# Taking the row maximum of attention scores over pairs of keys, with a ReLU on ScalarE and a joint add and maximum on VectorE

## What is computed

```python
def _L1_attn_ref(x, Wq, bq, Wk, bk, Wv, bv):
    q = jnp.einsum('bsd,ed->bse', x, Wq) + bq
    k = jnp.einsum('bsd,ed->bse', x, Wk) + bk
    v = jnp.einsum('bsd,ed->bse', x, Wv) + bv
    scale = 1.0 / jnp.sqrt(jnp.float32(x.shape[-1]))
    scores = jnp.einsum('bqd,bkd->bqk', q, k) * scale
    attn = jax.nn.softmax(scores, axis=-1)
    return jnp.einsum('bqk,bkd->bqd', attn, v)
...
x = x + _L0_conv_ref(_gn(x), L0_conv_weight)
t = _to_tokens(x)
t = t + _L1_attn_ref(_ln_t(t), ...)
t = t + _L1_ffn_ref(_ln_t(t), ...)
```

## Time and profile before

| | us |
|---|---|
| median of 3 runs | 3349.98 (3346.87 to 3349.98) |
| the profiled execution | 3355.51 |
| its span | 3353.4 |
| PE, DVE, ACT, POOL busy | 2829.6, 2110.8, 1417.5, 1017.1 |
| attention of the 56 chunks | about 204 to 2925 of the span |

### The profile page before, as it was taken

One profiled execution on the slowest core, in us unless ns is written; L12 is line 12 of the kernel. 1 busy time (PEld: TensorE's weight loads), 2 busy tenths in 40 slices (PEclk: granted clock), 3 DMA queues, 4 the chain that ended last, 5 costly groups with the idle time before them and its releaser, 6 DMA issues.

```text
span 3353.4 us, 46969 instructions
## 1 busy us (share of the span) xinstructions
PE 2829.6 (84%) x14124; PEld 1813.3 (54%) x14124; DVE 2110.8 (63%) x5723; ACT 1417.5 (42%) x3153; POOL 1017.1 (30%) x1185
## 2 busy tenths in 40 slices
PE   2489999999999999998999899998999898867660
PEld 1345555555666655655556566565665555545540
DVE  2466667667767777668666776777766766443331
ACT  0024443444454544554444454554455455523320
POOL 2000001222112224243242433423323432467445
PEclk9679999999999999999999999999999999955555
DMA  4100000001111111111111111111111111123321
GB/s 98 46 16 16 16 15 19 21 21 26 31 40 35 34 43 42 47 42 42 45 41 46 44 40 47 43 36 42 40 41 36 33 40 37 39 65 71 73 56 31
DMA packets 275327, 134.01 MB, mean 40 GB/s; under 512 B 225040, under 2 KB 268816, under 8 KB 275088
## 3 DMA queue, kind: packets, MB, share of 16 engines
q1 hardware_dynamic: 245168, 101.06, 12.2%
q0 software_dynamic: 29920, 29.94, 4.2%
HBM read 84.24 MB, written 46.66 MB: 39 GB/s over the span
## 4 chain that ended last, share of the span: by engine, by line
PE 61%; DVE 22%; issue 6%; POOL 5%; ACT 3%; DMA 2%; SPq 1%; POOLq 0%; DVEq 0%; ACTq 0%
PE ps_o L1095 16%; PE ps_s L1082 8%; DVE max_part L813 8%; PE ps_m L1061 8%; PE ps_z L1117 7%; PE ps_s L1084 6%; PE ps_x L1233 5%; POOL got L520 3%; PE ps_x L1248 2%; POOL sorted_x L507 2%; PE ps_z L1241 1%; PE ps_y L1167 1%; PE ps_z L1218 1%; DVE top_i L874 1%; DVE up L965 1%
## 5 line engine op out<-in xcount | busy, mean ns | idle before, releaser
L813 DVE TENSOR_REDUCE max_part<-ps_m 112x1 f32<-112x448 f32 x1568 | 942.0, 620 | 324.8 <-PE ps_m L1061 315.7
L637 ACT ACTIVATE prob<-ps_s 112x448 f32<-112x448 f32 x1568 | 849.1, 543 | 677.8 <-PE ps_s L1084 655.7
L1061 PE MATMUL ps_m<-k_a,q_a 128*112 128x448 f32 x1568 | 589.1, 394 | 146.7 <-DVE max_part L813 139.8
L1095 PE MATMUL ps_o<-prob,v_s 112*64 112x448 f32 x3136 | 690.5, 562 | 0.2 <-ACT prob L637 0.2
L1082 PE MATMUL ps_s<-q_a,k_a 128*112 128x448 f32 x1568 | 657.6, 419 | 16.4 <-ACT prob L637 10.2
L1084 PE MATMUL ps_s<-q_b,k_a 128*112 128x448 f32 x1568 | 573.8, 366 | 0.0
L507 POOL DMA_INDIRECT sorted_x<-row_now,slot_to x448 | 430.0, 960 | 167.3 <-issue 119.4
L520 POOL DMA_INDIRECT got<-sorted_y,slot_of x448 | 425.5, 950 | 163.9 <-issue 112.5
L530 POOL TENSOR_TENSOR ln_s<-ln_s,minus_half 112x4 f32<-112x4 f32 x56 | 58.0, 1036 | 1328.1 <-DVE ln_s L721 1328.1
L1061 PEld LDWEIGHTS ps_m<-k_a,q_a 128*112 128x112 f32 x1568 | 276.3, 176 | 316.9 <-DVE max_part L813 279.4
L1082 PEld LDWEIGHTS ps_s<-q_a,k_a 128*112 128x112 f32 x1568 | 276.3, 176 | 168.5 <-issue 102.9
(11 more groups left out here) (183 smaller groups left out, 3445.8 us busy)
## 6 DMA issues: line engine op xcount, KB each, us to landing
fx<-sorted_x SPq DMA_DIRECT2D x96, 192.0 KB
sorted_y<-fy SPq DMA_DIRECT2D x48, 320.0 KB, 3.0
fx<-sorted_x SPq DMA_DIRECT2D x112, 128.0 KB
x_st<-in_x SPq DMA_DIRECT2D x100, 112.0 KB, 2.8
xh<-in_x SPq DMA_DIRECT2D x80, 140.0 KB, 2.8
sorted_x<-row_now,slot_to POOLq DMA_INDIRECT x448
got<-sorted_y,slot_of POOLq DMA_INDIRECT x448
kept<-t_now SPq DMA_DIRECT2D x56, 112.0 KB, 1.9
```

Of the source, the lines that this page charges most:

```text
L637: a.activation(prob[(at.n * TILES + i) % PROBS][:], ps_s[i % 2][0:TILE, 0:CHUNK], ACT.Exp).then_inc(s["p_ready"], 1)
L813: v.tensor_reduce(max_part[:, m % PER, m // PER:m // PER + 1], ps_m[m % 2][0:TILE, 0:CHUNK], AX.X, ALU.max).then_inc(s["max_red"], 1)
L1061: t.matmul(ps_m[m % 2][0:TILE, 0:CHUNK], q_a[:, bass.ds(n % 2, 1), j * TILE:(j + 1) * TILE].rearrange("p a c -> p (a c)"), k_a[u % 2][:, k ...
L1095: t.matmul(ps_o[side:side + CHANNELS, 0:CHUNK], v_s[u % 2][:, i, :], prob[(n * TILES + i) % PROBS][:], start=(i < 2), stop=(i >= TILES - 2 ...
```

## The change

For two keys a and b, the larger of q·a and q·b is q·a + ReLU(q·(b - a)). The change uses this to halve what DVE reads.

DVE forms once for each chunk of keys the difference of its second and first 224 keys (`paired`, step 15, into the new buffers `k_d`). A maximum m now covers up to two chunks of keys: 4 blocks (`KEY_PAIRS`) times 4 tiles of queries, 16 in all (`MAXIMA`), of which the last four cover one chunk and are 224 wide. For each m, PE multiplies by the differences (`step`, L1095 of the new file, always into `ps_m[1]`) and by the first keys (L1109, always into `ps_m[0]`); ACT takes the ReLU of the first (`rises`, L641, into one of two buffers `above`); DVE does one `tensor_tensor_reduce` that adds the two and takes the maximum (L848). The difference of m + 1 is issued ahead of the first keys of m. It waits for the ReLU of m (`above_ready`), the first keys of m wait for the joint operation of m - 1 (`max_red`), and the ReLU of m waits for the difference of m and the joint operation of m - 2.

`max_reach` now spreads 16 over steps 2 to 24: one at each of the steps 2, 3, 4, 6, 7, 9, 10, 12, 13, 14, 16, 17, 19, 20, 22 and 23.

```diff
+            def rises(n, which):
+                for m in which:
+                    g, many, wide_ = key_pairs(m)
+                    act.wait_ge(s["step_done"], ONE + n * MAXIMA + m + 1)
+                    if n * MAXIMA + m >= 2:
+                        act.wait_ge(s["max_red"], ONE + n * MAXIMA + m - 1)
+                    a.activation(above[m % 2][:, 0:wide_], ps_m[1][0:TILE, 0:wide_], ACT.Relu).then_inc(s["above_ready"], 1)
...
                         act.wait_ge(s["s_done"], ONE + at.n * TILES + (i + 1))
                         a.activation(prob[(at.n * TILES + i) % PROBS][:], ps_s[i % 2][0:TILE, 0:CHUNK], ACT.Exp).then_inc(s["p_ready"], 1)
+                    if at.ahead:
+                        reach = max_reach(i)
+                        reach = min(reach + 1, MAXIMA) if reach else 0
+                        rises(at.n + 1, range(done, reach))
+                        done = reach
                     if i == Z_AFTER and at.active("post"):
...
+            def paired(at):
+                n, p, c = at.index("pre"), at.batch("pre") % 2, at.c
+                dve.wait_ge(s["k_ready"], ONE + n + 1)
+                v.tensor_tensor(k_d[p][:, c * HALF:(c + 1) * HALF], k_a[p][:, c * CHUNK + HALF:(c + 1) * CHUNK].bitcast(f32),
+                                k_a[p][:, c * CHUNK:c * CHUNK + HALF].bitcast(f32), ALU.subtract).then_inc(s["k_d_ready"], 1)
...
             def reduces(n, which):
                 for m in which:
-                    dve.wait_ge(s["max_done"], ONE + n * TILES + (m + 1))
-                    v.tensor_reduce(max_part[:, m % PER, m // PER:m // PER + 1],
-                                    ps_m[m % 2][0:TILE, 0:CHUNK], AX.X, ALU.max).then_inc(s["max_red"], 1)
+                    g, many, wide_ = key_pairs(m)
+                    dve.wait_ge(s["max_done"], ONE + n * MAXIMA + (m + 1))
+                    dve.wait_ge(s["above_ready"], ONE + n * MAXIMA + (m + 1))
+                    v.tensor_tensor_reduce(above[m % 2][:, 0:wide_], ps_m[0][0:TILE, 0:wide_], above[m % 2][:, 0:wide_],
+                                           1.0, LOWEST, ALU.add, ALU.max, max_part[:, m % PER, g:g + 1])\
+                        .then_inc(s["max_red"], 1)
...
+                def step(m):
+                    g, many, wide_ = key_pairs(m)
+                    if m == MAXIMA - PER:
+
+                        pe.wait_ge(s["k_d_ready"], ONE + (u + 1) * CHUNKS)
+                    if n * MAXIMA + m >= 1:
+                        pe.wait_ge(s["above_ready"], ONE + n * MAXIMA + m)
+                    t.matmul(ps_m[1][0:TILE, 0:wide_], mine(m), k_d[u % 2][:, g * CHUNK:g * CHUNK + wide_],
+                             start=True, stop=True).then_inc(s["step_done"], 1)
+
                 for m in which:
+                    g, many, wide_ = key_pairs(m)
                     if m == 0:
                         pe.wait_ge(s["qa_ready"], ONE + n + 1)
-                    if m >= 2:
-
-                        pe.wait_ge(s["max_red"], ONE + n * TILES + (m - 1))
...
+                        step(0)
+                    if m + 1 < MAXIMA:
+                        step(m + 1)
+                    if n * MAXIMA + m >= 1:
+                        pe.wait_ge(s["max_red"], ONE + n * MAXIMA + m)
+                    firsts = k_a[u % 2][:].rearrange("p (c h) -> p c h", h=CHUNK)[:, 2 * g:2 * g + many, 0:HALF]
+                    t.matmul(ps_m[0][0:TILE, 0:wide_], mine(m), firsts, start=True, stop=True).then_inc(s["max_done"], 1)
```

More of the change, by code:

```diff
@@ L54 @@
          (10, "post", "gate"), (11, "post", "picked"), (12, "post", "gate_exp"), (12, "pre", "apply1"),
-         (13, "post", "gates"), (14, "pre", "turned"), (19, "combine", "combine"), (21, "combine", "combined"), (21, "stats", "stats"),
+         (13, "post", "gates"), (14, "pre", "turned"), (15, "pre", "paired"), (19, "combine", "combine"), (21, "combine", "combined"), (21, "stats", "stats"),
          (22, "stats", "mean"), (23, "stats", "deviation"), (24, "stats", "variance"), (25, "stats", "scale")]
@@ L72 @@
 SHIFT = 26
+HALF = CHUNK // 2
+KEY_PAIRS = -(-CHUNKS // 2)
+MAXIMA = KEY_PAIRS * PER
+LOWEST = -3.0e38
 def wait_apart(engine, sem, value):
@@ L223, in build @@
         prob = [sb(f"prob{i}", [TILE, CHUNK]) for i in range(PROBS)]
-        max_part = sb("max_part", [TILE, PER, CHUNKS])
+        k_d = [sb(f"k_d{p}", [128, TOKENS // 2], f32r) for p in range(2)]
+        above = [sb(f"above{i}", [TILE, CHUNK]) for i in range(2)]
+        max_part = sb("max_part", [TILE, PER, KEY_PAIRS])
         max_neg = sb("max_neg", [TILE, PER])
@@ L309, in tiles, with key_pairs @@
             return bass.ds(c * PER, PER)
+        def key_pairs(m):
+            g = m // PER
+            many = min(2, CHUNKS - 2 * g)
+            return g, many, many * HALF
         def wide(ap, shape):
@@ L633, in body @@
             def body(at):
+                done = 0
                 for i in range(TILES):
@@ L654, in body @@
                     next_queries(0)
+                    rises(0, range(MAXIMA))
                     next_shift(0)
@@ L984, in _ @@
             events = {"normed": normed, "convolved": conv, "norm1": norm1,
-                      "apply1": apply1, "residual": attended, "rows": rows, "norm2": norm2, "apply2": apply2, "picked": gate,
+                      "apply1": apply1, "paired": paired, "residual": attended, "rows": rows, "norm2": norm2, "apply2": apply2, "picked": gate,
                       "gates": gates_of, "combine": combine,
@@ L1018, in body @@
                     next_queries(0)
-                    reduces(0, range(TILES))
+                    reduces(0, range(MAXIMA))
                     max_total(0)
@@ L1047, in maxima, with mine @@
             def maxima(n, u, which):
+                def mine(m):
+                    return q_a[:, bass.ds(n % 2, 1), m % PER * TILE:(m % PER + 1) * TILE].rearrange("p a c -> p (a c)")
+                def step(m):
[6 more added lines that the diff above has]
+                             start=True, stop=True).then_inc(s["step_done"], 1)
                 for m in which:
+                    g, many, wide_ = key_pairs(m)
                     if m == 0:
                         pe.wait_ge(s["qa_ready"], ONE + n + 1)
-                    if m >= 2:
-                        pe.wait_ge(s["max_red"], ONE + n * TILES + (m - 1))
[L1055 to L1058, removed]
-                        pe.wait_ge(s["k_ready"], ONE + (u + 1) * CHUNKS)
-                    t.matmul(ps_m[m % 2][0:TILE, 0:CHUNK],
-                             q_a[:, bass.ds(n % 2, 1), j * TILE:(j + 1) * TILE].rearrange("p a c -> p (a c)"),
-                             k_a[u % 2][:, kb * CHUNK:(kb + 1) * CHUNK], start=True, stop=True).then_inc(s["max_done"], 1)
+                        pe.wait_ge(s["k_d_ready"], ONE + (u + 1) * CHUNKS - 1)
+                        step(0)
[5 more added lines that the diff above has]
+                    t.matmul(ps_m[0][0:TILE, 0:wide_], mine(m), firsts, start=True, stop=True).then_inc(s["max_done"], 1)
             def shift(n):
@@ L1301, in body @@
                     queries(0, 0, 0)
-                    maxima(0, 0, range(TILES))
+                    maxima(0, 0, range(MAXIMA))
                     bank_y.take()
```

10 lines of the change are left out of this document (5 added, 5 removed).

## The result

Both kernels on the same chip: 3407.85 us after (median of 4, 3406.06 to 3409.96) against 3348.43 us before (3345.63 to 3349.98). The ratio is 1.0181, with a 95% interval of 1.0168 to 1.0194. The forecast was 3390 us, +1.2%, with a range of 3315 to 3485. The profiled execution has a span of 3408.2 us against 3353.4, that is +54.8 where the sum of the prediction gave +42.

The account below looks back on a forecast made before the run. The prediction took PE (TensorE) to be the bound. Its terms 122 + 8 + 73 - 161 gave +42 us; 3355.5 + 42 - 5.5 = 3392, said as 3390 us, +1.2%, range 3315 to 3485.

Parts of the forecast that it names:

- Part 1: DVE's work: 28 reductions a chunk give way to 16 joint operations with read-outs; DVE gets 5.5 us a chunk back.
- Rival (c): On DVE: the joint operation runs at half rate, 1.08 us; +170 us, 3560 us in all; chance 0.08.
- Part 3: ACT's work: 16 ReLUs a chunk add 6.3 us there, hidden by volume on an engine busy for 42%.
- Part 4: Steps 2 to 4: single-depth banks delay `xg_f` and the convolution, net 2.3 to 2.55 us a chunk; +122 us together.
- the sign: At step 4: the first-keys matmul is ended by the joint operation, with 0.9 us or more of idle.
- part 5: Short new PE waits at steps 7, 13, 17, 20 and 23: 1.5 us a full chunk, 0.8 an early one; +73 us.
- part 6: What comes back on PE: most waits for reductions, restart costs and half the 47.3 us for `xn`; -161 us.
- part 2: PE's work: 32 matmuls a chunk for 28, same columns, about +0.15 us a chunk; +8 us over 55 chunks.
- the moved matmuls: Three matmuls of a chunk, 0.6 us, only move ahead of the convolution; taken off the front's delay.
- the prologue: Its serial pass: 28 rounds of 0.7 against 16 of about 1.25, put at nothing.
- Rival (a): Behind step 5: DVE relief wins, part 5 is nil and the `xn` wait goes whole; -54, 3296 us; chance 0.22.
- Rival (b): Whole kernel: gains and losses cancel, with part 5 at 0.6 us a chunk; within 7 us of 3350; chance 0.10.

Follow-up runs that it names:

- experiment 1: Changed kernel with the next image's normalization (`xg_f`, `xg_hi`, `xg_lo`) at step 1 instead of step 2: 3334.22 us, ratio 0.9956 to the kernel before.
- experiment 3: Changed kernel with the difference matmul of maximum 0 and its ReLU in step 1 instead of step 2: 3360.08 us, ratio 1.0033 to the kernel before.
- experiment 4: Changed kernel with both moves, those of experiment 1 and experiment 3: 3291.50 us, ratio 0.9825 to the kernel before.
- experiment 7: Kernel before with one bank for its 28 maxima instead of two, each matmul waiting for the reduction just ahead: 3951.73 us, ratio 1.1803.
- experiment 6: Changed kernel with its 16 maxima from step 5 on instead of step 2 (`MAX_FROM` 5): 3470.75 us, ratio 1.0368 to the kernel before.
- experiment 8: Kernel before with 28 maxima, first keys and differences in one matmul, ReLU and join of 224, two alternating banks, normalization in step 1: 3360.15 us, ratio 1.0038.

## Why the prediction was right, point by point

**Part 1 (DVE's work)** held: 0.62, 0.39 and 0.08 us for the three new rows were forecast as 0.63, 0.4 and 0.08. The sum's 0.62 a round is right only as the time until the next operation can start, read-out included: from 2051.01 to 2051.55 and on to 2051.64 it was 0.63. By the rows it is 942 - 601 = 341 us less, for 340 forecast. The busy table shows 377; it counts the overlap of an operation and its read-out once. Rival (c), half rate, is out at 622 ns. The rule of the Trainium skill that was weighed there (page "Vector Engine (DVE) Microarchitecture Reference", section "Points that are easy to get wrong") doesn't bite with one source in PSUM, and the trace agrees: an accumulating operation on PSUM and SBUF in float32 ran in the time of a plain one.

**Part 3 (ACT's work)**: 446.2 us by rows (546 ns and 354 ns), 313 by the busy table, for some 420 forecast. By volume it hides, as said. The relu rule of the Trainium skill (page "ScalarE: Activation LUTs", section "Rules for kernel authors") gives its factor for bf16. For float32 out of PSUM the traces show nothing like it: 546 ns for the ReLU on ACT, 620 for a reduction of 448 elements on DVE; no run here put the ReLU on DVE.

**Part 4 (the front)** is the best part of it. Walked against the trace by the offset of the first ReLU (2047.03 for 1983.05), the forecast has the second difference at 2047.6 (measured 2047.62), `xg_f` at 2048.96 (2048.98), first-keys 2 at 2051.8 (2051.69) and the convolution at 2052.8 (2052.71). The table above doesn't take off the 0.6 us of the three matmuls that have only moved into the front, so it is to be held against 2.9 a late chunk and 3.15 an early one: 14 x 3.15 + 35 x 2.9 + 6 x 1.6 = 155 us. Measured 162.2, of which 12 are the convolution at the lower clock; without them it is 150, or 3.0 for an early chunk and 2.83 for a late one. Experiments 1 and 3 took the chain's two links out, each with about its price. Only the sign that I had named for it was off: 0.9 us or more of idle ahead of first-keys 2. It is 0.49, and 0.20 more ahead of the difference before it.

**The term that was missing** is the clock, on both sides of the sum: +12 us in the convolutions up to chunk 14, and some -17 behind the front, where the kernel before had its falls. It all but cancels, and that is luck: the prediction looked at neither. The traces of experiments 1 and 4, without the stops of step 4, have no convolution at the lower clock in the attention; the changed kernel has some 70 matmuls of them, and experiment 3 has 20.

**Parts 5 and 6 and part 2** fall into the same steps. Together they were forecast as 8 + 73 - 161 - 33 (the moved matmuls) = -113 us, measured -111.9. The idle rows tell part of it apart. Ahead of the maximum matmuls of steps 5 to 27, 128 us of idle time went, as part 6 had it, and 42 us in 113 pieces came or stayed; with 0.25 more for each piece (an estimate, see experiment 7) that is 70 us for the 73 of part 5. But this total is right by luck: it is 2.3 us in an early chunk for 0.8 forecast, and 0.9 in the others for 1.5. The early chunks' step 13 alone costs 1.5 us more, their step 17 0.7, and steps 14 and 15 gave back 1.9; the late ones' step 13 costs 0.25 for 0.6 forecast. In part 6, the wait for `xn` gave back 11 us (47.3 to 36.1) for 24, and the clock's 17 weren't in it; these parts don't add up to the measured sum exactly. Of the late steps, 15 and 21 gave most: 2.33 to 0.67 and 4.54 to 2.81. The stops of the earlier trace rows are gone but for small ones; this is what is left of them in step 20 of chunk 37:

```profile
2083.37 0.36 PE L1095 MATMUL ps_m<-k_d,q_a 128*112 128x224 f32 x1 [0.27 <-ACT above L641]
```

An image's first chunk, from chunk 21 on, gained more than the others, 53.07 to 50.86, where I had put the relief lower by 5 us over all. Some 1.8 of these 2.2 us are the clock, by the same estimate: it fell in all five of these chunks before, and in two of them now.

**Rival (a)** was to show by less than 60 us of PE idle ahead of the two maximum lines; it was 90.4 + 55.5 = 146. **Rival (b)** needed part 5 at 0.6 a chunk. The total was 55 by the spans for a forecast of 42: 7 more in the front, 1 more behind it, 4.1 for the prologue, which I had put at nothing, and 0.4 for the tail. So the mechanism of the front was foreseen and holds, and the closeness of the total owes something to errors that cancel.

## What to carry to other kernels

When buffers that took turns are given one each to two kinds of product, the rounds in flight fall to one; price that by following one chunk's chain through every engine, as in part 4, and not by the engines' busy shares. Look above all at where the new operation stands in the queue of a helping engine ahead of something that the bound waits for: here ScalarE was busy for 51% only, and yet its ReLUs and the waits for them cost 110 us; moving two entries of the order turned +1.8% into -1.75%. Spreading work that has one buffer evenly (experiment 6), or splitting it to have two buffers again (experiment 8), can both lose more than it gives; my reading of both is that the spacing of the rounds counts against the length of the longest one. And look at the granted clock in the kernel before as well as in the one after: a fall that shows in the new place may have gone from an old one.

## What the runs showed of the hardware that I had not expected

- The granted clock fell to 0.51 behind stops of only 0.88 and 0.48 us whose ends lay 0.94 us apart (and one of 0.86, 3.1 us earlier), and stayed there for 7 to 10 of the dense matmuls behind them; in the next chunk the same three stops left it at full speed. Each time cost 1.5 us. The kernel before did the same behind stops of 0.71 and 1.04 us in chunk 29, and not behind 0.70 and 1.04 in chunk 30. Experiment 3, without the stop of 0.86, has it in three chunks for eight. What decides was not tried and stays open.
- An add with a running maximum, PSUM and SBUF sources, float32, takes 622 ns for 448 elements and 388 for 224, as a reduction or a plain add of that width; the row that writes the maximum out takes 83 ns.
- A stop of PE seems to cost some 0.25 us more than the idle time that its row shows: this is an estimate from the rows around a stop, and the growth of step 2 fits it. In experiment 7 it accounts for some 130 of the 263 us that came without an idle row, and the lower clock, by estimate, for some 140.
